# Order of the last two units' transposes and copies in the second and third attention of a four-layer kernel

## What is computed

```python
x = layernorm(x + attention(x))
x = layernorm(x + ffn(x))
```

```python
s = q @ k.T * scale + bias_and_mask    # one head, 256 queries, 256 keys
p = exp(s - max(s)); o = (p @ v) / sum(p)
x = x + concat(o) @ Wo
```

## Time and profile before

| | |
|---|---|
| median of 3 runs | 3066.17 us (3064.02 to 3066.51) |
| profiled execution | 3065.75 us, of which the span on the engines 3063.9 us |
| busy over the span | PE 2431.1 us (79%), DVE 1999.3 (65%), POOL 1428.3 (47%), ACT 1365.4 (45%) |
| TensorE clock granted, mean | 0.925 of full speed |
| second attention, 835.60 to 1121.00 us | PE 232.17, DVE 244.96, ACT 154.71, POOL 225.20 us busy of 285.40, clock 1.00 |
| third attention, 1477.00 to 1767.00 us | PE 260.25, DVE 233.92, ACT 174.98, POOL 209.15 us busy of 290.00, clock 1.00 |

### The profile page before, as it was taken

The page is one execution under the profiler, slowest core; times in us unless marked ns, Lnnn a source line. Parts: engine busy times, 40 slices in busy tenths (PEclk is TensorE's granted clock), DMA queues, the critical chain, the costliest instruction groups (busy, mean ns, idle before and its releaser), DMA issues. The chain is left out here.

```text
span 3063.9 us, 73428 instructions
## 1 busy us (share of the span) xinstructions
PE 2431.1 (79%) x21502; PEld 1851.7 (60%) x21503; DVE 1999.3 (65%) x8520; ACT 1365.4 (45%) x3166; POOL 1428.3 (47%) x1621
## 2 busy tenths in 40 slices
PE   5888888687788870863998859984898899999977
PEld 4666666454456540542776747772776677777755
DVE  3666666545588863225888858986565577767746
ACT  1333333322455540322666625651554566666633
POOL 2666666300588744015777706551332345445511
PEclk7999999889899995986999979996999999999978
DMA  2000000033000002111000010000000000000000
GB/s 66 2 1 0 0 0 0 19 84 104 11 1 0 0 9 81 36 44 51 2 0 0 0 36 2 1 0 0 2 0 8 14 2 0 0 0 0 0 1 28
DMA packets 40528, 46.25 MB, mean 15 GB/s; under 512 B 6072, under 2 KB 30514, under 8 KB 40117
## 3 DMA queue, kind: packets, MB, share of 16 engines
q1 hardware_dynamic: 38332, 40.34, 4.6%
q0 software_dynamic: 2048, 4.20, 0.5%
HBM read 34.41 MB, written 10.12 MB: 15 GB/s over the span
## 5 line engine op out<-in xcount | busy, mean ns | idle before, releaser
L1080 POOL TENSOR_TENSOR a_sm<-a_sm,a_top 128x512 f32<-128x512 f32 x576 | 586.7, 1040 | 289.3 <-DVE a_top L883 289.3
L1003 ACT ACTIVATE a_pr<-a_sm 128x512 f32<-128x512 f32 x576 | 355.0, 627 | 273.1 <-POOL a_sm L1080 168.2
L883 DVE CUSTOM_DVE_ANT_0 a_sm<-bank,cst 128x256 f32<-128x256 f32 (+1 forms) x1024 | 301.2, 353 | 117.6 <-PE bank L745 117.5
L759 PE MATMUL bank<-cst,a_pr 128*128 128x128 f32 x2304 | 306.7, 276 | 0.7 <-ACT a_pt L1013 0.4
L2892 POOL TENSOR_TENSOR a_pr<-a_sm,a_rden 128x512 f32<-128x512 f32 x192 | 197.1, 1047 | 225.9 <-DVE a_rden L2678 225.5
L891 DVE COPY a_pt<-bank 128x512 f32<-128x512 f32 x288 | 198.1, 688 | 139.8 <-PE bank L759 137.0
L759 PEld LDWEIGHTS bank<-cst,a_pr 128*128 128x128 f32 x2304 | 258.2, 142 | 29.7 <-issue 20.3
L1013 ACT ACTIVATE a_pt<-bank 128x512 f32<-128x512 f32 x288 | 169.1, 587 | 99.5 <-PE bank L759 95.6
L2652 DVE CUSTOM_DVE_ANT_0 a_sm<-bank,cst 128x256 f32<-128x256 f32 (+1 forms) x512 | 149.8, 353 | 51.0 <-PE bank L2539 43.6
L779 PEld LDWEIGHTS bank<-a_pt,a_v 128*32 128x32 f32 x4608 | 118.9, 110 | 103.4 <-issue 88.3
L779 PE MATMUL bank<-a_pt,a_v 128*32 128x128 f32 x4608 | 156.1, 276 | 21.1 <-ACT a_pt L1013 8.8
(11 more groups left out here) (473 smaller groups left out, 6063.1 us busy)
## 6 DMA issues: line engine op xcount, KB each, us to landing
f_spread<-gate_rows SPq DMA_DIRECT2D x16, 512.0 KB, 7.6
W<-in_l_w SPq DMA_DIRECT2D x2, 2048.0 KB, 9.8
x_sorted<-p_zero SPq DMA_DIRECT2D x4, 768.0 KB, 5.4
f_xin<-x_sorted SPq DMA_DIRECT2D x12, 256.0 KB, 2.8
y_sorted<-f_yout SPq DMA_DIRECT2D x10, 256.0 KB, 2.3
X<-in_x SPq DMA_DIRECT2D x4, 512.0 KB, 8.3
a_bias<-bias_rows SPq DMA_DIRECT2D x1, 2048.0 KB, 8.0
out_x<-X SPq DMA_DIRECT2D x8, 256.0 KB, 2.3
```

What stands on the lines that cost most here:

```text
L759: mm = pe.transpose(tbank[j % 2][:, c * P:(c + 1) * P], pr[j][:, c * P:(c + 1) * P], ident)
L883: ins = dve.tensor_tensor_reduce(sm[j][:, m * kw:(m + 1) * kw], sbank[j][:, m * kw:(m + 1) * kw], mk, 1.0, 3.0e38, ALU.add, ALU.min, top[: ...
L1003: act.activation(pr[j][:, :], sm[j][:, :], ACT.Exp, scale=-1.0).then_inc(S["probs"], 1)
L1080: pool.tensor_tensor(whole, whole, top[:, qt, a:a + m].unsqueeze(2).to_broadcast([P, m, kw]), ALU.subtract).then_inc(S["shifted"], 1)
```

## The change

On PE, for `lanes == 1`, turns 2 and 3 move from behind the groups of denominators and repeated reciprocals to ahead of them; they stay behind the projection. On DVE, the copy of unit 3 (`copies(i, s, (2, 3))`, of which DVE has unit 3) moves from behind reciprocal, norm and `keep_moments` to a place between the residual and the reciprocal. ACT's and POOL's orders stay. No instruction and no wait is added or removed.

```diff
@@ tensor, slot @@
                 if in_loop(i):
                     steps_in(i, s, 2)
+                if lanes == 1:
+                    for q in lagging(i, s, LT):
+                        turn(i, q, 2)
+                        turn(i, q, 3)
                 for e in ending(i, s, LD):
                     denominators(i, s, e)
...
                 if lanes == 2:
                     for e in ending(i, s, LY):
                         project(i, s, e)
-                for q in lagging(i, s, LT):
-                    turn(i, q, 2)
-                    turn(i, q, 3)
+                    for q in lagging(i, s, LT):
+                        turn(i, q, 2)
+                        turn(i, q, 3)
@@ vector, slot @@
                 if lanes == 1:
                     for e in ending(i, s, LY):
                         residual(i, e)
+                    copies(i, s, (2, 3))
                 for e in ending(i, s, LD):
                     recip(i, e)
...
                     steps_in(i, s, 2)
-                copies(i, s, (2, 3))
+                if lanes == 2:
+                    copies(i, s, (2, 3))
```

## The result

The changed kernel took 3079.09 us in the median (3076.53 to 3083.16, 5 runs), the kernel before 3066.17 (3064.02 to 3066.55, 5 runs on the same chip). The ratio is 1.0046 (95% interval 1.0031 to 1.0061), so +12.9 us where +4.2 on the median was forecast. It lies above the range. The profiled execution took 3082.04 us, span 3080.3; the one of before 3065.75 and 3063.9.

The account below looks back on a forecast made before the run. Next scores wait for residual, reciprocal and norm, so DVE replaces PE as limit; POOL's chain ends last in the second attention. 13 x 0.37 = +4.8, 13 x 0.03 = +0.4, ends -0.6: +4.6, giving 3070.4 us; range 3061 to 3075.5.

Parts of the forecast that it names:

- The PE's 0.88 us given to DVE whole: Third attention: PE could start scores 0.88 us earlier, but DVE's later norm takes it all; C 7.24 against 7.23.
- C: Slot with s mod 3 = 0 (repeated reciprocals, projection, step q); third attention forecast 7.24 us, 7.23 before.
- Reciprocal and norm 0.60 later: DVE, each slot: copy 3 now precedes reciprocal and norm, making both 0.60 us later, counted from the masks.
- A: Slot with s mod 3 = 1 (projection, denominators, step k); forecast 6.59 us in both attentions, 5.99 and 6.17 before.
- The norm's wait, 0.15 us: From the norm's end on DVE to PE's next scores: 0.15 us taken, between bounds of none and 0.25.
- B: Slot with s mod 3 = 2 (denominators, repeated reciprocals, step v); forecast 6.56 us in second attention, 6.88 in third.
- The first rival: Scores after the norm: the wait costs 0.25 us instead of 0.15, in 39 waits; slower, 3075.2 us; chance 0.23.
- The copy of moments waits for POOL: DVE, second attention, A: the copy waits for POOL's running instruction to end, taking about 0.58 us instead of 0.17.
- The second rival: Copy of moments on DVE doesn't stretch at its new place, so step k is on time: 3065.0 us; chance 0.13.
- the statistics and the k product behind it start at 6.95: DVE, second attention, A: work behind the copy of moments starts at 6.95 instead of 6.53 us, 0.42 late.
- The ends, -0.5 in each attention: Loop draining: norm and L809 no longer precede the last copy 3; one of the two counted, -0.5 us per attention.
- The third rival: Third attention, B and C: scores need not follow the norm, each 0.88 us shorter; faster, 3052.6 us; chance 0.12.

Follow-up runs that it names:

- The kernel with two buffers: Changed kernel with two buffers for the moments, so the statistics wait for the last aggregation, not the copy of moments: 3070.3 us, ratio 1.0013.
- the second measurement: The changed kernel run once more, unaltered, for a second profile beside another run on the same chip: 3076.56 us, ratio 1.0034.

## Why the prediction was wrong

- **The PE's 0.88 us given to DVE whole:** right. C of the third attention took 7.22, forecast 7.24. PE's order by itself costs nothing; alone it gives -17.5 us.
- **Reciprocal and norm 0.60 later:** right. A took 6.58 in both attentions, forecast 6.59; the third attention's period is 20.66, forecast 20.71.
- **The norm's wait, 0.15 us:** chosen without a row, and so partly luck. It was 0.14 to 0.15 after the norms of C and of every second B, and 0.05 to 0.06 after the other Bs (957.34 against 956.92 + 0.36). The first rival (0.25) did not occur, and the slower result is not its doing.
- **The copy of moments waits for POOL:** right, 0.57 for 0.58. The second rival falls. In the second attention all 28 of these copies before and all 27 after ended within 0.03 us of the end of a POOL instruction. The exclusive lock that the Trainium skill describes ("SBUF — State Buffer", section "Who interferes with whom") agrees with that.
- **The step that failed** is the next one: "the statistics and the k product behind it start at 6.95". They start at 6.96 and 7.17, that is, the statistics where I had the product. I had gone through what the moved instructions wait for, not through what waits for them once they are neighbours. `tile_stats` waits for `moments_kept`; with copy 3 between them that wait was always over. Its price of 0.23 us was put at nothing, though the trace of before had one of its kind: in the third attention the aggregation waits for the statistics just ahead of it, 4.1 us in 27 places, 0.15 each beyond the end of the statistics.

```profile
DVE a_mv L917 <- DVE a_stat L912: 4.1, 27, 0.2
```

  Over 13 periods the wait is 3.0 us. The kernel with two buffers took it away and had the forecast's period.
- **What was missing altogether:** stretches at half clock. I looked at the granted clock of the second attention (1.00 over 285 us) and took it as given for the changed kernel, though the change moves idle time of PE. At three or four stretches of 1.5 us it is 4.6 to 6 us, and the median's 12.9 is near 4.6 + 3.0 + 4.6 = 12.2. Near and no more: the second measurement gave +10.6, with four stretches in its profile. Either term alone would have left the forecast time inside the range (3073.4 and 3075.0); both together, 3078.0, lie above it. The range had no case for the clock. Why it falls in some slots and not in others stays open.
- **The ends, -0.5 in each attention:** from the last scores to the last projection the third attention took 0.8 less than before. The second took as long as before in the repeated profile (16.84 against 16.83) and 1.4 longer in the first, where the clock fell there too.
- **The third rival** (the PE's gain arrives, about 3053) does not hold for this change. The gain itself was there to be had: with DVE's order left alone 3047.6, and with the copy of moments out of the way too 3037.5.

## What to carry to other kernels

When work moves on an in-order engine, list the pairs that become neighbours, and look for a wait of the second on the first: an instruction that used to stand between them may have paid for it. Before two moves on two engines are made together, ask of each what waits for it last: here the scores waited for norm and reciprocal, and copy 3 had time to spare, so only the PE half was worth having. Put small copies that can be held up by POOL where their engine is idle, not ahead of a product that feeds POOL.

## What the runs showed of the hardware

- DVE's copy of 128x2 numbers from SBUF to SBUF took 0.17 to 1.05 us in the second attention of the kernel before and 0.57 to 0.83 after. It ended within 0.03 us of the end of a POOL instruction each time. The reciprocal (0.25), the statistics (0.28 to 0.29) and the copies out of PSUM (0.68 to 0.69) kept their length beside POOL.
- A DVE instruction that waits by semaphore for the one just ahead of it started 0.15 us after its end; without the wait 0.08 before it. The difference is 0.23 us, and two buffers gave back 0.25 in each period (20.94 to 20.69).
- TensorE's granted clock fell to its lower level in the middle of a stage in which PE was busy for 83% of the time (229.32 of 276.97 us), with waits of 0.91 and 0.79 us just ahead, and four small transposes in that idle time kept it up at no cost there (one profile).
